# Delta-rule layer in a Trainium2 decoder: chunk solves in four quadrants of the matmul array, with half of the key copies moved by DMA

## The chip, the cores and the metric

One Trainium2 chip, one of its cores. The metric is the device time of one execution of the whole program, in microseconds (us), shown as the median of 3 runs.

## What is computed

The reference is a two-layer decoder on x of 4 sequences x 512 tokens x 128. Each of its six blocks adds its output to x and normalises. The change touches the fourth block only, the delta rule (a linear attention with 16 heads of width 64 and a state matrix W per head):

```python
Q = (x @ Wq).reshape(B, T, H, D)
K = (x @ Wk).reshape(B, T, H, D)
V = (x @ Wv).reshape(B, T, H, D)
beta = jax.nn.sigmoid(x @ Wbeta + b_beta)
K = K / jnp.maximum(jnp.linalg.norm(K, axis=-1, keepdims=True), EPS)
def step(W, inp):
    q_t, k_t, v_t, b_t = inp
    pred = jnp.einsum('bhij,bhj->bhi', W, k_t)
    err = v_t - pred
    W_new = W + b_t[..., None, None] * jnp.einsum('bhi,bhj->bhij', err, k_t)
    o_t = jnp.einsum('bhij,bhj->bhi', W_new, q_t)
    return (W_new, o_t)
```

After it come a cross attention (stage E in the kernel) and a mixture of experts (stage F).

## The kernel before

The kernel runs six stages, A to F. In stage D (the delta rule, from about 1085 us to 1590 us of the span) the 512 tokens of a sequence are cut into 8 chunks of 64, and the recurrence is solved chunk by chunk with matmuls. The work comes in 16 **units** u = 0 to 15; a unit is four heads (two pairs of heads) of one sequence with all 8 chunks. Two units share one **key set** m = u // 2 (eight heads).

For a unit, `d_prep_tensor` (L1747) issues on TensorE, in steps that end in `yield`: values and queries, the `corner` and `fold` products that finish the inverse of each 64x64 chunk matrix, `products` (L1765), four `solve` steps (L1795), then four `update` steps (L1807): transitions "da", steps "db", reads "dr", outputs "do". A solve multiplies the inverse of one chunk (tile d_XE) with the 128 columns of that chunk's values and keys (tile d_KV): 8 chunks x 4 heads = 32 matmuls of 64x64 by 128 columns a unit, in fp32; the trace records each fp32 matmul twice, so it shows 64. Even chunks (`half` 0) lie on partitions 0 to 63, odd ones on 64 to 127. In `solve(k)` a matmul reads the partitions of its half and writes PSUM partitions of the same half, so that two 64x64 quadrants of the array, those on its diagonal, can be at work; `k` runs over two pairs p and two heads `par` of a pair, and each k fills one PSUM bank. ScalarE copies each bank to d_UW (`d_prep_scalar`, L1863, wait at L1893). The updates and `products` take their matmuls in the order of TILES (L1461), in which four successive matmuls use four different quadrants; in the updates a PSUM bank takes the matmuls of one row half.

The banks of this stage come from a ring of five (`ringD`, L1458; class Ring, L91): a step that takes a bank waits until the copy out of its last use is done. `d_chain_tensor` (L1971) carries the state d_S from chunk to chunk: a matmul pair per chunk, an addition on VectorE, the next matmul pair.

The order on each engine is set by `weave` (L35), which merges streams of steps in proportion to their lengths, and by `d_order` (L2051), which says which streams run in an **iteration** u: the chain of unit u, the preparation of unit u+1, and others. Odd iterations (1, 3, 5, 7, 9) also hold the key rows of a later key set, with a Newton square root in small operations on VectorE (`d_rows_vector`, L1596); they prepare units 2, 4, 6, 8, 10. Even iterations 2 to 10 hold key transposes (ident x d_KV into d_KT) and Gram products (d_KT x d_KT) of `d_turn_tensor` (L1543); they prepare units 3, 5, 7, 9, 11. Iterations 11 and 12 hold neither; 13 to 15 hold the start of stages E and F. GpSimd inverts 32x32 blocks (`d_inverse_gpsimd`, L1727), one key set in two iterations.

SyncE issues every DMA, in program order. In stage D it issues, per key set, one reset of d_XI with the unit matrix (`d_inverse_sync`, L1684, loop at L2620); after all eight of them `e_load_sync` (L2138: 7 loads of stage E, once unit 11's outputs are used, semaphore d_out) and `f_load_sync` (L2144). TensorE's first use of the stage E loads is in `e_first_tensor` (L2152), the first step of iteration 13.

## Time and profile before

| | |
|---|---|
| median of 3 runs | 1722.1 us (1721.47 to 1723.83) |
| the profiled execution's own time | 1721.14 us |
| its span | 1719.4 us |
| TensorE busy (matmuls) | 1501.6 us, 87% of the span |
| VectorE busy | 1212.3 us, 71% |
| ScalarE busy | 910.1 us, 53% |
| GpSimd busy | 694.4 us, 40% |
| DMA, mean over the span | 41 GB/s |
| mean granted TensorE clock | 0.946 of full speed |

The profiled execution is 1.0 us under the median. Busy shares are averages over stages with different limits; what a change to stage D is worth has to be read from the stretches in which it runs. In the views below, PE is TensorE, DVE is VectorE, ACT is ScalarE, POOL is GpSimd and SP is SyncE; "ps" is PSUM; an arrow points from the inputs to the output.

### The profile page before, as it was taken

How to read it: one execution, taken by the hardware profiler on the slowest of the kernel's cores; microseconds unless marked ns; L12 is line 12 of the kernel's file. 1: busy time of each engine (PE TensorE's matmuls, PEld its weight loads, DVE VectorE, ACT ScalarE, POOL GpSimd, SP SyncE). 2: the span in 40 equal slices, each digit the busy share in tenths (PEclk: the TensorE clock that was granted, in tenths of full speed). 3: DMA queues.
4: the chain of work that ended last, by engine and by line, in shares of the span. 5: the costliest groups of instructions: out<-in, count | busy, mean ns of one | idle time of the engine just before them, and what ended most of it. 6: DMA issues, size and time to landing. Idle time of an engine off the chain costs nothing.

```text
span 1719.4 us, 41752 instructions
## 1 busy us (share of the span) xinstructions
PE 1501.6 (87%) x18044; PEld 808.2 (47%) x18044; DVE 1212.3 (71%) x2245; ACT 910.1 (53%) x1269; POOL 694.4 (40%) x732
## 2 busy tenths in 40 slices
PE   8887888999999999999978877888889899898985
PEld 4222223333334334333424544777777687664442
DVE  7889877988757774767617668575776666474766
ACT  1676675777757675876671433554445544342220
POOL 1111031566555554665570107447675556000000
PEclk8899999999999999999998989999999999879998
DMA  4000003332222331422301000000000001000000
GB/s 154 1 1 1 1 1 111 100 86 80 80 72 71 84 102 38 106 84 72 88 15 64 1 1 13 15 16 16 3 15 16 15 4 51 37 2 1 7 7 13
DMA packets 32408, 70.65 MB, mean 41 GB/s; under 512 B 5328, under 2 KB 7056, under 8 KB 31968
## 3 DMA queue, kind: packets, MB, share of 16 engines
q1 hardware_dynamic: 32224, 67.98, 13.7%
q8 instruction: 142, 2.33, 0.6%
q14 instruction: 42, 0.34, 0.1%
HBM read 47.45 MB, written 20.51 MB: 40 GB/s over the span
## 4 chain that ended last, share of the span: by engine, by line
PE 57%; DVE 28%; ACT 8%; issue 6%; POOL 1%; DMA 0%; SPq 0%; ACTq 0%; DVEq 0%; POOLq 0%
PE ps L159 55%; DVE a_MX L407 5%; DVE b_mx L863 2%; ACT b_X L923 1%; PE ps L227 1%; PE ps L1551 1%; DVE st L171 1%; DVE sq L206 1%; ACT d_L L168 1%; DVE b_rd L1033 1%; DVE b_VL L798 1%; DVE d_XE L1674 1%; DVE d_KV L1628 1%; POOL b_EL L941 1%; DVE st L197 1%
## 5 line engine op out<-in xcount | busy, mean ns | idle before, releaser
L941 POOL TENSOR_TENSOR b_EL<-b_X,b_EH 128x1024 f16<-128x1024 f32 x160 | 341.2, 2133 | 235.5 <-ACT b_EH L168 235.5
L923 ACT ACTIVATE b_X<-ps 128x1024 f32<-128x1024 f32 x160 | 163.6, 1022 | 118.6 <-PE ps L159 117.2
L1737 POOL TENSOR_TENSOR d_tmp<-d_G,d_XI 128x31 f32<-128x31 f32 (+15 forms) x248 | 128.5, 518 | 194.4 <-DVE d_G L1666 175.6
L863 DVE TENSOR_REDUCE b_mx<-ps 128x2 f32<-128x1024 f32 x128 | 156.0, 1219 | 52.4 <-PE ps L159 50.7
L168 ACT ACTIVATE b_EH<-b_X 128x1024 f16<-128x1024 f32 x160 | 169.1, 1057 | 34.4 <-PE ps L159 23.2
L159 PE MATMUL ps<-b_M,b_S 128*128 128x512 f16 (+1 forms) x768 | 178.4, 386 | 2.4 <-ACT b_X L923 2.4
L407 DVE TENSOR_REDUCE a_MX<-ps 128x2 f16<-128x1024 f32 x128 | 155.3, 1226 | 28.8 <-PE ps L159 27.5
L444 ACT ACTIVATE a_E<-ps 128x1024 f32<-128x1024 f32 x128 | 131.1, 1024 | 77.1 <-PE ps L159 76.4
L1740 POOL TENSOR_TENSOR d_XI<-d_XI,d_tmp 128x31 f32<-128x31 f32 (+15 forms) x248 | 140.8, 568 | 19.4
L426 POOL TENSOR_TENSOR a_QS<-a_QS,a_MR 128x512 f16<-128x512 f16 x16 | 18.5, 1154 | 217.2 <-ACT a_MR L168 213.2
L159 PEld LDWEIGHTS ps<-b_M,b_S 128*128 128x128 f16 (+1 forms) x768 | 55.3, 98 | 101.2 <-issue 40.4
L2474 POOL TENSOR_TENSOR f_Y<-X,f_bo 128x512 f32<-128x512 f32 x4 | 6.1, 1534 | 210.2 <-DVE X L219 112.7
L159 PE MATMUL ps<-b_Hk,b_Hq 64*128 64x154 f16 (+1 forms) x512 | 67.7, 312 | 16.0 <-DVE b_mx L863 15.0
L159 PE MATMUL ps<-f_XM,f_Wh 128*128 128x512 f16 x256 | 78.0, 387 | 0.0
L159 PE MATMUL ps<-a_QS,a_KS 32*128 32x512 f16 x256 | 51.9, 402 | 29.4 <-DVE a_MX L407 29.1
L159 PE MATMUL ps<-d_KV,d_XE 64*64 64x128 f32 x1024 | 72.9, 290 | 1.5 <-issue 1.4
L168 ACT ACTIVATE d_UW<-ps 128x512 f32<-128x512 f32 x64 | 38.2, 597 | 67.3 <-PE ps L159 67.3
L159 PE MATMUL ps<-a_E,a_VA 128*32 128x512 f32 x512 | 73.2, 645 | 0.3
L1346 ACT ACTIVATE c_SG<-ps 128x512 f32<-128x512 f32 x36 | 21.5, 597 | 92.0 <-PE ps L159 88.4
L159 PE MATMUL ps<-b_EH,b_VH 128*64 128x512 f16 x320 | 65.6, 406 | 5.0 <-ACT b_OT L168 2.5
L1002 DVE TENSOR_TENSOR b_den<-b_den,ps 128x512 f32<-128x512 f32 x44 | 30.1, 684 | 51.6 <-PE ps L159 51.3
L159 PEld LDWEIGHTS ps<-b_Hk,b_Hq 64*128 64x128 f16 x512 | 19.9, 94 | 98.3 <-issue 46.7
(324 smaller groups left out, 3435.0 us busy)
## 6 DMA issues: line engine op xcount, KB each, us to landing
b_S<-s_xk SPq DMA_DIRECT2D x48, 336.0 KB, 6.5
b_M<-s_xq SPq DMA_DIRECT2D x48, 256.0 KB, 5.1
s_xk<-b_Hk SPq DMA_DIRECT2D x16, 336.0 KB, 2.2
s_xk<-b_Lk SPq DMA_DIRECT2D x16, 336.0 KB, 2.4
s_xq<-b_Hq SPq DMA_DIRECT2D x16, 256.0 KB, 2.0
s_xq<-b_Lq SPq DMA_DIRECT2D x16, 256.0 KB, 2.0
d_XI<-eye SPq DMA_DIRECT2D x8, 512.0 KB, 3.6
f_w<-f_w SPq DMA_DIRECT2D x1, 2048.0 KB, 7.9
```

Source lines behind the costliest of these rows:

```text
L159: return e.matmul(out, lhsT, rhs, start=start, stop=stop, skip_group_check=True)
L168: return e.activation(out, a, ACT.Copy)
L407: v.e.tensor_reduce(out, PS[:, bk:bk + 2, :], AX, ALU.max).then_inc(sem("a_mx"), 1)
L426: p.e.tensor_tensor(a_QS[G % 4], a_QS[G % 4], a_MR[G % 2], ALU.add).then_inc(sem("a_q2"), 1)
L444: a.e.activation(a_E[c][:, 2 * hp:2 * hp + 2, :], PS[:, bk:bk + 2, :], ACT.Exp, scale=float(D) ** -0.5).then_inc(sem("a_ex"), 1)
L863: last = v.e.tensor_reduce(b_mx[:, 0, :, n], PS[:, bk:bk + 2, :], AX, ALU.max)
L923: a.e.activation(b_X[k % 2], PS[:, bk:bk + 2, :], ACT.Exp, scale=0.125).then_inc(sem("b_ex"), 1)
L941: last = p.e.tensor_tensor(b_EL[k % 6], b_X[k % 2], b_EH[k % 6], ALU.subtract)
L1002: last = v.e.tensor_tensor(b_den[b % 2], b_den[b % 2], PS[:, bk, :], ALU.add)
L1346: a.e.activation(c_SG[n % 3], PS[:, bank["cgu", b, p], :], ACT.Silu).then_inc(sem("c_sl"), 1)
L1737: e.tensor_tensor(tm, a, x, ALU.mult).then_inc(*p.step())
L1740: last = e.tensor_tensor(z, z, tm, ALU.subtract)
```

## The change

- `solve` takes a pair of heads at once: two banks, one per head, and per chunk pair four matmuls in the four quadrants. The first head's results lie as before; the second head's (`par` 1) lie with their halves swapped: even chunks on partitions 64 to 127, odd ones on 0 to 63. There are two solves a unit in place of four, each of 32 / 2 = 16 matmuls with a `yield` in its middle.
- The semaphore d_um rises by 2 a unit and not by 4. ScalarE waits for a whole pair and then makes its two copies.
- `products` writes the second head's results with swapped halves too, and the updates read swapped halves. The four quadrants of an update stay four different ones; their order changes, and a bank now takes matmuls of both row halves.
- The updates' keys of the second heads must lie swapped as well: a new tile d_KW (4 KB on each partition, one buffer) is filled once per key set by `d_swap_sync`: 8 DMAs from SBUF to SBUF, each 64 partitions x 4 heads x 64 words, 64 in all. SyncE waits before them for the keys (d_kn), for the previous key set's last use in "db" (d_bm) and for c_dm.
- TensorE waits for d_kw ahead of the transitions of each key set.
- On SyncE the swap of key set m stands behind the reset of d_XI of key set m + 2, and the last two swaps stand ahead of the loads of stages E and F.
- d_KW takes the place of two buffers of f_XM of stage F; those move to words 5124 on, where the query weights were, with a wait for all queries (d_qm).

```diff
+        d_KW = Room(nc, 34468).take("d_KW", 1024).rearrange("p (c a n) -> p c a n", c=4, a=4)
...
-            v.wait_ge("d_um", 8 * m)
+            v.wait_ge("d_um", 4 * m)
...
+        def d_swap_sync(s, m):
+
+            s.wait_ge("d_kn", 4 * m + 4)
+            s.wait_ge("d_bm", 2 * m)
+            s.wait_ge("c_dm", 16)
+            for c in range(4):
+                for half in range(2):
+                    dma(s.e, "d_kw", d_KW[HALF[1 - half], c], d_KV[m % 3][HALF[half], c, 1, 1:8:2, :])
...
-                    last = mm(e, PS[HALF[half], bk[par], o:o + 64], KT[HALF[par], 2 * j + p, tok(c, half)],
+                    last = mm(e, PS[HALF[half ^ par], bk[par], o:o + 64], KT[HALF[par], 2 * j + p, tok(c, half)],
...
-            def solve(k):
-                par, p = k // 2, k % 2
-                bk = ringD.take(t, ("du", u, k), 1, "d_u", 4 * u + k + 1)
+            def solve(p):
+                bk = [ringD.take(t, ("du", u, p, par), 1, "d_u", 4 * u + 2 * p + par + 1) for par in range(2)]
...
                 for c in range(4):
-                    for half in range(2):
-                        last = mm(e, PS[HALF[half], bk, 128 * c:128 * c + 128], X[HALF[half], at_chunk(p, c, par), :],
+                    for half, par in ((0, 0), (1, 0), (0, 1), (1, 1)):
+                        last = mm(e, PS[HALF[half ^ par], bk[par], 128 * c:128 * c + 128], X[HALF[half], at_chunk(p, c, par), :],
                                   KV[HALF[half], c, :, 4 * j + head(p, par), :])
+                    if c == 1:
+                        yield
                 last.then_inc(sem("d_um"), 1)
+                yield
...
-                        last = mm(e, PS[HALF[par], bk[half], o:o + 64], *operands(HALF[half], p, c, par))
+                        last = mm(e, PS[HALF[par], bk[half], o:o + 64], *operands(HALF[half ^ par], p, c, par))
...
             def keys_of(r, p, c, par):
-                return KV[r, c, 1, 4 * j + head(p, par), :]
+                return d_KW[r, c, 2 * j + p, :] if par else KV[r, c, 1, 4 * j + head(p, par), :]
...
-            for k in range(4):
-                solve(k)
-                yield
-            yield
+            for p in range(2):
+                yield from solve(p)
+            yield
+            t.wait_ge("d_kw", 128 * (m + 1))
             update("da", "d_a", "d_am", 64, 128, 1, 6, transitions)
...
-            for k in range(4):
-                a.wait_ge("d_um", 4 * u + k + 1)
-                copy(e, d_UW[:, 4 * k:4 * k + 4, :],
-                     PS[:, bank["du", u, k], :].rearrange("p (i n) -> p i n", i=4)).then_inc(sem("d_u"), 1)
-                yield
+            for p in range(2):
+                a.wait_ge("d_um", 2 * u + p + 1)
+                for par in range(2):
+                    i = at_chunk(p, 0, par)
+                    copy(e, d_UW[:, i:i + 4, :],
+                         PS[:, bank["du", u, p, par], :].rearrange("p (i n) -> p i n", i=4)).then_inc(sem("d_u"), 1)
+                    yield
...
-        for k, word, n in ((0, 36516, 4), (0, 34468, 2), (0, 6148, 2), (1, 13604, 8)):
+        for k, word, n in ((0, 36516, 4), (0, 6148, 2), (0, 5124, 2), (1, 13604, 8)):
...
+                if k == 6:
+                    v.wait_ge("d_qm", 2 * NU)
...
-            for m in range(NH):
-                d_inverse_sync(s, m)
+            for m in range(NH + 2):
+                if m < NH:
+                    d_inverse_sync(s, m)
+                if m > 1:
+                    d_swap_sync(s, m - 2)
```

Three places of the instruction order, before and with the change.

TensorE in iteration 2, where unit 3's solves (d_KV, d_XE) stand among key transposes (ident, d_KV) and Gram products (d_KT). Before:

```order
L1551 MATMUL ps<-ident,d_KV_189 128x128 x4
L159 MATMUL ps<-d_KV_188,d_XE 64x128 [waits d_pt]
L159 MATMUL ps<-d_KV_188,d_XE 64x128 x7
L1551 MATMUL ps<-ident,d_KV_189 128x128 [waits d_pt]
L1551 MATMUL ps<-ident,d_KV_189 128x128 x3
L159 MATMUL ps<-d_KT_191 64x64 [waits d_kt,d_u]
L159 MATMUL ps<-d_KT_191 64x64 x31
...
L159 MATMUL ps<-d_KT_191 64x64 [waits d_kt,d_g]
L159 MATMUL ps<-d_KT_191 64x64 x31
L159 MATMUL ps<-d_KV_188,d_XE 64x128 [waits d_g]
L159 MATMUL ps<-d_KV_188,d_XE 64x128 x7
```

With the change:

```order
L1552 MATMUL ps<-ident,d_KV_189 128x128 [waits d_pt]
L1552 MATMUL ps<-ident,d_KV_189 128x128 x3
L159 MATMUL ps<-d_KV_188,d_XE 64x128 x8
L1552 MATMUL ps<-ident,d_KV_189 128x128 [waits d_pt]
L1552 MATMUL ps<-ident,d_KV_189 128x128 x3
L159 MATMUL ps<-d_KT_191 64x64 [waits d_kt,d_u]
L159 MATMUL ps<-d_KT_191 64x64 x31
...
L159 MATMUL ps<-d_KT_191 64x64 [waits d_kt,d_g]
L159 MATMUL ps<-d_KT_191 64x64 x31
L159 MATMUL ps<-d_KV_188,d_XE 64x128 x8
```

Each group of 8 solve matmuls stays where it was; eight of them are now two fours of quadrants, and the Gram products still wait for a copy d_u and the copies d_kt.

ScalarE at the same place: copies of transposed keys (d_KT) and of solved chunks (d_UW), then the block copies of d_L. Before:

```order
L168 ACTIVATE d_KT_191<-ps 128x512 [waits d_ptm,d_gm,d_ktp]
L168 ACTIVATE d_UW<-ps 128x512 [waits d_um]
L168 ACTIVATE d_KT_191<-ps 128x512 [waits d_ktp]
L168 ACTIVATE d_UW<-ps 128x512 [waits d_um]
L168 ACTIVATE d_KT_191<-ps 128x512 [waits d_ktp] x2
L168 ACTIVATE d_UW<-ps 128x512 [waits d_um] x2
L168 ACTIVATE d_L_193<-d_L_193 32x32x32 [waits d_g]
```

With the change:

```order
L168 ACTIVATE d_KT_191<-ps 128x512 [waits d_ptm,d_gm,d_ktp]
L168 ACTIVATE d_UW<-ps 128x512 [waits d_um]
L168 ACTIVATE d_KT_191<-ps 128x512 [waits d_ktp]
L168 ACTIVATE d_UW<-ps 128x512
L168 ACTIVATE d_KT_191<-ps 128x512 [waits d_ktp] x2
L168 ACTIVATE d_UW<-ps 128x512 [waits d_um]
L168 ACTIVATE d_UW<-ps 128x512
L168 ACTIVATE d_L_193<-d_L_193 32x32x32 [waits d_g]
```

The order is the same; the first and the third copy of d_UW now wait for a whole pair, so the second d_KT copy stands behind a wait for 16 matmuls and not for 8.

SyncE's queue ahead of the loads of stage E, as a piece of the difference:

```order
+L174 DMA d_KW<-d_KV_187 64x4x64 [waits d_bm,d_kn]
+L174 DMA d_KW<-d_KV_187 64x4x64 x7
+L174 DMA d_KW<-d_KV_189 64x4x64 [waits d_bm,d_kn]
+L174 DMA d_KW<-d_KV_189 64x4x64 x7
+L174 DMA d_KW<-d_KV_188 64x4x64 [waits d_bm,d_kn]
+L174 DMA d_KW<-d_KV_188 64x4x64 x7
 L174 DMA e_wy<-y_wy 128x128 [waits d_out]
 L174 DMA e_cT<-ctx_T 128x616
```

The load of e_wy stood behind the last reset of d_XI; it now stands behind the swap of key set 7, whose wait d_bm is for unit 13.

## Rows read from the trace of the kernel before

**Rows 1.** The page: busy time of the engines, and the chain that ended last.

```profile
PE 1501.6 (87%) x18044; PEld 808.2 (47%) x18044; DVE 1212.3 (71%) x2245; ACT 910.1 (53%) x1269; POOL 694.4 (40%) x732
...
PE 57%; DVE 28%; ACT 8%; issue 6%; POOL 1%; DMA 0%; SPq 0%; ACTq 0%; DVEq 0%; POOLq 0%
```

**Rows 2.** Stretches: length, busy PE, PEld, DVE, ACT, POOL, then PEclk, DMA share, GB/s.

```profile
1200.00:1300.00 100.00, 89.12 (x2624) 73.70 (x2622) 68.85 (x151) 49.06 (x85) 62.61 (x112) 0.98 0.03 9
1524.40:1537.60 13.20, 13.09 (x109) 8.36 (x107) 10.98 (x29) 7.47 (x15) 0.00 (x0) 0.50 0.00 1
```

**Rows 3.** Tile d_KV: all solve matmuls, duration min/median/max in ns.

```profile
L159 PE MATMUL ps<-d_KV,d_XE x1024: 267/269/473, 1095.0 to 1535.5; 64*64 64x128 f32 x171
```

**Rows 4.** Timeline of TensorE in iteration 4 (unit 5): start, length in us, operation.

```profile
1233.02 1.09 PE L159 MATMUL ps<-d_KV,d_XE 64*64 64x128 f32 x16
...
1236.23 1.16 PE L159 MATMUL ps<-d_KT 64*64 64x64 f32 x64
...
1242.05 0.94 PE L159 MATMUL ps<-d_KV,d_UW 64*64 64x64 f32 x48 [0.32 <-ACT d_UW L168]
...
1246.75 2.05 PE L159 MATMUL ps<-d_wo,d_OT 128*128 128x128 f32 x16
```

**Rows 5.** Timeline of ScalarE in the same iteration.

```profile
1234.16 0.60 ACT L168 ACTIVATE d_UW<-ps 128x512 f32<-128x512 f32 x1 [0.43 <-PE ps L159]
...
1235.77 0.60 ACT L168 ACTIVATE d_UW<-ps 128x512 f32<-128x512 f32 x1 [0.43 <-PE ps L159]
...
1241.31 0.60 ACT L168 ACTIVATE d_UW<-ps 128x512 f32<-128x512 f32 x1 [1.21 <-PE ps L159]
1241.80 2.11 ACT L168 ACTIVATE d_L<-d_L 32x1024 f32<-32x1024 f32 x2
```

**Rows 6.** Timeline of TensorE in iteration 5 (unit 6).

```profile
1268.26 1.92 PE L159 MATMUL ps<-d_KV,d_XE 64*64 64x128 f32 x32
1270.71 0.45 PE L159 MATMUL ps<-d_S,d_AT 64*64 64x64 f32 x8 [0.54 <-DVE d_S L2017]
```

**Rows 7.** Timeline of VectorE in iteration 5: the two idle times around the solves.

```profile
1263.18 0.69 DVE L1610 TENSOR_REDUCE d_z<-d_sqk 128x8 f32<-128x512 f32 x1 [1.46 <-ACT d_sqk L1575]
...
1281.59 0.76 DVE L171 SCALAR_TENSOR_TENSOR d_KV<-ps,d_sb 128x256 f32<-128x256 f32 x2 [0.91 <-PE ps L159]
```

**Rows 8.** Timeline of TensorE in iteration 11 (unit 12).

```profile
1428.44 1.85 PE L159 MATMUL ps<-d_KV,d_XE 64*64 64x128 f32 x30
...
1431.17 0.93 PE L159 MATMUL ps<-d_KV,d_UW 64*64 64x64 f32 x48 [0.31 <-ACT d_UW L168]
```

**Rows 9.** Units 0 and 1: TensorE's solves of unit 0, VectorE ahead of unit 1's transitions.

```profile
1095.03 4.95 PE L159 MATMUL ps<-d_KV,d_XE 64*64 64x128 f32 x64
...
1129.38 1.15 DVE L1953 TENSOR_TENSOR d_AT<-d_id,ps 128x192 f32<-128x192 f32 x4 [0.83 <-PE ps L159]
```

**Rows 10.** TensorE from unit 13's steps to the first use of stage E's loads.

```profile
1454.15 0.22 PE L159 MATMUL ps<-d_UW,d_KV 64*64 64x64 f32 x1
...
1459.29 0.68 PE L159 MATMUL ps<-e_cT,e_wy 128*128 128x308 f32 x2
...
1461.90 0.79 PE L159 MATMUL ps<-e_cT,e_wy 128*128 128x308 f32 x2 [1.92 <-ACT d_OT L168]
```

**Rows 11.** SyncE's issues: start and length on the queue, or ns min/median/max.

```profile
1436.92 0.33 SPq L174 DMA_DIRECT2D e_wy<-y_wy  x1
...
1439.90 0.43 SPq L174 DMA_DIRECT2D e_mr<-mask_r  x1
...
L174 SPq DMA_DIRECT2D b_S<-s_xk x48: 574/607/1446, 271.2 to 843.6; - x48
```

**Rows 12.** DMA view of 1436 to 1443 us: packets, MB, share of 16 engines; a load's landing.

```profile
q1 hardware_dynamic: 1008, 0.89, 46.9%
...
e_mr<-mask_r SPq DMA_DIRECT2D x1, 308.0 KB, 3.0
```

**Rows 13.** VectorE in iteration 4: the second transpose that frees a reset of d_XI.

```profile
1250.60 1.22 DVE L1674 STREAM_TRANSPOSE d_XE<-d_XI 128x512 f32<-128x512 f32 x1
```

More of the change, by code:

```diff
@@ L30 @@
     "f_bm": ("a_oc", 16), "f_xm": ("a_pv", 64),
-    "d_inv": ("a_ws", 4), "d_x1": ("b_kv", 6), "d_btm": ("b_kt", 6), "xr_E": ("xr_A", 4), "xr_F": ("xr_B", 4), "f_wh": ("d_wh", 3),
+    "d_inv": ("a_ws", 4), "d_x1": ("b_kv", 6), "d_btm": ("b_kt", 6), "xr_E": ("xr_A", 4), "xr_F": ("xr_B", 4), "f_wh": ("d_wh", 3), "d_kw": ("b_pm", 144),
 }
```

## The prediction

> **What bounds the kernel now.** I read the page first: TensorE is busy 87% of the span and carries 57% of the chain that ended last, VectorE 28% [rows 1]. That is an average. In a stretch of stage D alone TensorE is busy 89 of 100 us, VectorE 69, ScalarE 49, GpSimd 63 [rows 2], so TensorE time looks worth saving; but every engine waits in turn for another there, because the order is fixed and a chunk's results pass from TensorE over ScalarE or VectorE back to TensorE. What a shorter solve is worth must therefore be read unit by unit: which wait ends last behind the solves. For that I went through the timelines of TensorE, ScalarE and VectorE around the solves of all 16 units.
>
> **The solves themselves.** Sixteen records, which are 8 matmuls or 4 diagonal pairs, take 1.09 us, the last of them a duration of 0.27 [rows 3, 4]: (1.09 - 0.27) / 4 = 0.205 us a pair. Thirty-two records give the same, (1.92 - 0.27) / 8 = 0.206 [rows 6]. That two do run side by side is seen beside full-array fp32 matmuls of the same 128 columns, 8 in 2.05 us, 0.22 to 0.25 each [rows 4]. Four quadrants at once are shown by the Gram products: 32 matmuls of 64 columns in 1.16 us, eight fours of about 0.12 [rows 4]. A four of 128 columns thus costs between 0.205 (the pair's rate) and 2 x 0.12 = 0.24; I take 0.21, since the pair has the same columns. A unit goes from 16 x 0.205 = 3.3 us to 8 x 0.21 = 1.7 us (at the other end 1.9): 1.6 us less, 26 us over 16 units. The rest of the working is what of this reaches the end.
>
> **What gives it back: the last copy.** The transitions wait for all four d_UW copies. Before, one copy was left when the last solve ended; now two are, and the second starts some 0.57 us later (copies of 0.60 us, one behind the other [rows 5]). So a unit in which nothing else binds gains 1.6 - 0.6 = 1.0 us.
>
> **Unit by unit.**
> - Units 12 and 13: no key rows, no transposes; TensorE waits 0.31 us for d_UW ahead of the transitions and for nothing else [rows 8]. 1.0 us each: 2.0 (ends 1.6 and 3.0).
> - Units 3, 5, 7, 9, 11, among the transposes. First solve piece at 1233.02, Gram product at 1236.23 [rows 4]. The second piece was done when the second d_UW copy began, at 1235.77 [rows 5]; both pieces shrink by 0.41 us, so it is now done at about 1234.9. ScalarE's first d_UW copy, at 1234.16 before [rows 5], waits for that and stands ahead of the second d_KT copy, which follows 0.57 us later and ends at 1236.05; the Gram product waits for it: about 0.2 us earlier than before, not 1. The same happens in the second half; d_L's copies, which VectorE and the reads wait for, start behind the last d_UW copy (1241.31 before) [rows 5]. I get 0.3 us a unit, 1.5 in all (ends 0 and 5).
> - Units 2, 4, 6, 8, 10, beside the key rows. VectorE has no idle time listed from 1263.18 to 1281.59, a stretch that encloses unit 6's solves; TensorE even waits 0.54 us for an addition that is queued behind VectorE's Newton steps [rows 6, 7]. A faster solve there makes that wait longer. 0.2 a unit, 1.0 in all (ends 0 and 5).
> - Unit 0: 64 records take 4.95 us, as its first part ran at the lower clock [rows 3, 9]; half of that less 0.6 is 1.8 (ends 1.0 and 2.0). Unit 1: VectorE idles only 0.83 us ahead of the transitions [rows 9], so 0.8 at most; I take it (other end 0.4).
> - Unit 14: two normalisation and softmax chains of stage E lie around it; 0 (other end 0.8).
> - Unit 15: TensorE is busy 13.09 of 13.20 us at a granted clock of 0.50, the lower of the two levels, 1.2 GHz; VectorE is busy 10.98 [rows 2]. Its solves cost twice as much and halve to about 3.6 us less, but VectorE has just 2.2 us to give, and ScalarE's mask copies now queue between the two last d_UW copies. 1.5 (ends 0 and 3).
>
> Sum of the gains: 2.0 + 1.5 + 1.0 + 1.8 + 0.8 + 0 + 1.5 = 8.6 us.
>
> **The DMAs.** The swap of a key set is 8 issues on SyncE. No row shows an issue of 64 x 4 pieces; a plain load's takes 0.33 to 0.43 us, and the nearest, a 64 x 2 x 1344 one, has a median of 0.607 and a maximum of 1.446 [rows 11]. I take 0.6, the row nearest in shape. The data are 2048 packets of 256 bytes, 128 on each of 16 engines. Loads of mixed sizes took 0.469 x 7 x 16 / 1008 = 0.052 us a packet [rows 12], so at most some 6.7 us, overlapped with the issues. A swap can start when VectorE's second transpose has freed d_XI, at about 1251.8 [rows 13], and unit 6's transitions come near 1271: 19 us of cover against 0.33 + 8 x 0.6 + 3 = 8 us, and 15 us at the dearest issue. Cost nothing. If that cover were gone, TensorE would stand at d_kw with everything behind it.
>
> **Where a queue does cost: the loads of stage E.** Before, they were issued from 1436.92 to 1440.3, the last landing 3.0 us later [rows 11, 12], far ahead of their first use at 1459.29 [rows 10]. Now the swap of key set 7 stands ahead of them, and it waits for unit 13's steps, which end at 1454.4 [rows 10]. With an issue cost x the loads land at 1454.4 + 8x + 3.4 (their own seven issues) + 3.0. TensorE and VectorE both stand there; nothing between the steps and that use gets shorter. The second of these matmuls before had to wait until 1461.90 anyway, for a bank [rows 10]; that part of the stall was already paid. The net loss is (1454.4 + 8x + 6.4 + 0.65) - 1461.9 = 8x - 0.45: at x = 0.6 4.4 us, at 0.33 2.2, at 1.446 11.1. The loads of stage F follow a few us later and are used 50 us on: nothing. The two moved f_XM buffers wait for queries that are issued before: nothing.
>
> **The sum.** 8.6 - 4.4 = 4.2 us less than the profiled execution's 1721.1, 1716.9. The median of the runs is 1.0 us above that execution; on its scale I predict **1718 us**.
>
> **Rivals.**
> 1. *The load queue eats the gain* (the slower side). One mechanism: SyncE's eight issues ahead of the stage E loads. From x = (8.6 + 0.45) / 8 = 1.1 us an issue the change is no gain; at 1.446 and gains of 3 to 8 us it ends at 1724 to 1730. For it: the four 256-byte pieces per partition; the maximum of the nearest row. Against: its median. 0.25.
> 2. *The units beside key rows and transposes gain more*, because VectorE's and ScalarE's work moves up with TensorE's. At 0.8 a unit in place of 0.2 and 0.3, 5 to 6 us more: 1712. For it: those engines are idle at many other places. Against: the waits of [rows 5 to 7]. 0.20.
> 3. *The four quadrants don't run four wide.* A bank now takes both row halves at once, in the solves and the updates. If they then ran in pairs, solves would stay as they are, and an update of 24 matmuls, 0.94 us now [rows 4], would double: about 3 us a unit, 1722 + 16 x 3 = 1770. Against: the solves of before put both halves into one bank, and paired [rows 3, 4]. This is a rule of the Trainium skill, TensorEngine Tiling (Array Packing), section Restrictions and Gotchas: "Different row tiles cannot access same PSUM bank simultaneously", with the synchronisation left to software. The trace of before disagrees as far as timing goes, for two quadrants; no row shows four with two banks. 0.05.
> 4. *The swaps land late* for the transitions. It takes 2 us or more an issue; every further us is paid seven times. 1730 and up. 0.04.
>
> **How the numbers follow.** The forecast, some 3 to 8 us faster or near it, has 0.46; its own range is 1713 to 1721. The measurement tells 0.2% (3.4 us) from no change, so faster is below 1718.7 and slower above 1725.5. Of the forecast's 0.46 I put 0.28 below 1718.7, with rival 2 that makes 0.48; slower has 0.05 + 0.04 and 0.13 of rival 1, 0.22; the rest, 0.30, is the same. The bounds would reach from 1722.1 - 20 + 2.2 = 1704 to 1722.1 - 3 + 11.1 = 1730; leaving out the outermost parts and rivals 3 and 4, the range is 1709 to 1728.
>
> **What the profile after would show.** Solve records: 64 in about 2 us of TensorE time a unit in place of 3.5, and the updates' 24 matmuls still 0.94 us (if 1.8, rival 3). Behind the solves of units 12 and 13 the wait for d_UW should be 0.7 to 0.9 us and not 0.31. In iteration 4 TensorE should wait ahead of the Gram product for d_KT, and in iteration 5 for d_S. SyncE's rows give x directly, and the wait for the loads of stage E should be 5 to 7 us once; none for d_kw. The prediction is wrong if x is far from 0.6, if units beside key rows gain more than 0.5 us each, or if a new wait shows at each key set.

## The result and the profile after

| | before | after |
|---|---|---|
| median of the runs | 1722.1 us (5 runs, 1720.32 to 1724.11) | 1731.2 us (5 runs, 1729.90 to 1732.03) |
| profiled execution, span | 1719.4 us | 1728.1 us |
| mean granted TensorE clock | 0.946 | 0.942 |

The ratio is 1.0057, with a 95% interval of 1.0045 to 1.0070: slower by some 9 us, where I had forecast 4 faster. A second measurement, with 12 runs (below), gave 1.0039 (1.0021 to 1.0056).

The page of after, busy times and chain, against [rows 1]:

```profile
PE 1482.0 (86%) x18044; PEld 785.3 (45%) x18044; DVE 1212.5 (70%) x2245; ACT 905.9 (52%) x1269; POOL 695.7 (40%) x732
...
PE 53%; DVE 28%; ACT 8%; issue 7%; POOL 3%; DMA 1%; SPq 1%; ACTq 0%; DVEq 0%; POOLq 0%
```

TensorE is busy 19.6 us less, from 1501.6, and its share of the chain falls from 57% to 53%. The work did get shorter; the span did not. So waits grew by more than the work shrank, and GpSimd, a DMA and SyncE's queue stand in the chain with 3, 1 and 1%.

**Where it went.** The most useful yardstick was the start of each unit's `d_AT` subtraction on VectorE, which is one event per unit. The differences between such starts, from the profiles of before and after:

| stretch | before | after | after less before | forecast |
|---|---|---|---|---|
| start to unit 0 | 1101.74 | 1099.98 | -1.8 | -1.8 |
| unit 0 to 2 | 58.69 | 59.60 | +0.9 | -1.0 |
| unit 2 to 11 | 249.36 | 249.76 | +0.4 | -2.3 |
| unit 11 to 13 | 43.48 | 42.20 | -1.3 | -2.0 |
| unit 13 to 14 | 40.71 | 48.87 | +8.2 | +4.4 |
| unit 14 to 15 | 45.80 | 46.77 | +1.0 | -1.5 |
| unit 15 to the end | 179.6 | 180.9 | +1.3 | 0 |

A stretch between two such starts holds the work of the later unit. The last two columns add up to +8.7 and -4.2 us.

How far can one profile be trusted? Five kernels (some of them described below) have the same TensorE work up to unit 13 (after and runs 1, 3, 9 and 10). Their profiles give 248.9 to 250.1 us for units 2 to 11, but 41.5 to 44.7 us for units 11 to 13. The latter goes with the clock: from unit 11 to 12 they took 21.1 to 21.4 us where the granted clock was 1.00, 23.0 us at 0.85 and 24.4 us at 0.79. Before took 22.4 us there at 0.92, after 21.1 at 1.00, so part of the -1.3 us is the clock. The start of unit 0 lies between 1096.0 and 1100.2 us in these five, so the -1.8 us in the first line is no measurement of unit 0.

Two things are to be explained: nine units with 1.6 us less TensorE work each that gain nothing, and 8 us lost at one place.

**Nine units that gain nothing.** Groups of TensorE's instructions between the subtractions of units 2 and 11 (busy, mean ns, idle time before them and its releaser). Before:

```profile
L159 PE MATMUL ps<-d_KV,d_XE 64*64 64x128 f32 x576 | 37.2, 272 | 0.7 <-issue 0.7
...
L159 PE MATMUL ps<-d_S,d_AT 64*64 64x64 f32 x432 | 23.7, 226 | 5.1 <-DVE d_S L2017 2.9 <-issue 1.8
...
L159 PE MATMUL ps<-d_KT 64*64 64x64 f32 x640 | 11.6, 221 | 0.0
...
L159 PE MATMUL ps<-d_KV,d_UW 64*64 64x64 f32 x432 | 8.7, 222 | 1.8 <-ACT d_UW L168 1.6
```

After:

```profile
L159 PE MATMUL ps<-d_S,d_AT 64*64 64x64 f32 x432 | 24.1, 227 | 11.0 <-DVE d_S L2031 9.5 <-issue 1.0
L159 PE MATMUL ps<-d_KV,d_XE 64*64 64x128 f32 x576 | 22.7, 276 | 0.4 <-issue 0.4
...
L159 PE MATMUL ps<-d_KT 64*64 64x64 f32 x640 | 11.6, 221 | 4.5 <-ACT d_KT L168 4.5
...
L159 PE MATMUL ps<-d_KW,d_UW 64*64 64x64 f32 x216 | 9.4, 222 | 4.2 <-ACT d_UW L168 4.2
```

The solves fell from 37.2 to 22.7 us, 14.5 / 9 = 1.6 us a unit, as forecast. What came back: the recurrence's waits for `d_S` +6.6, the Gram products' for `d_KT` +4.5 (from none), the updates' for `d_UW` +2.6 (from 1.6). That is 13.7 of the 14.5 us. These are idle times before TensorE's instructions, and not yet causes: the experiments show that the first of the three comes with any shorter solve, and only the other two with the late signal (table behind run 7).

Iteration 4 shows how, on ScalarE of after, against [rows 5]:

```profile
1233.79 0.60 ACT L168 ACTIVATE d_UW<-ps 128x512 f32<-128x512 f32 x1 [1.22 <-PE ps L159]
1234.29 0.59 ACT L168 ACTIVATE d_KT<-ps 128x512 f32<-128x512 f32 x1
1234.76 0.60 ACT L168 ACTIVATE d_UW<-ps 128x512 f32<-128x512 f32 x1
1235.24 0.62 ACT L168 ACTIVATE d_KT<-ps 128x512 f32<-128x512 f32 x1
1237.26 0.60 ACT L168 ACTIVATE d_KT<-ps 128x512 f32<-128x512 f32 x1 [1.40 <-PE ps L1552]
1239.66 1.08 ACT L168 ACTIVATE d_UW<-ps 128x512 f32<-128x512 f32 x2 [1.80 <-PE ps L159]
```

ScalarE idles 1.22 us at the first `d_UW` copy with a `d_KT` copy queued behind it. TensorE, on its side, then stands for that `d_KT` (timeline of the same iteration, against [rows 4]):

```profile
1231.87 0.67 PE L159 MATMUL ps<-d_KV,d_XE 64*64 64x128 f32 x16
...
1233.06 0.67 PE L159 MATMUL ps<-d_KV,d_XE 64*64 64x128 f32 x16
...
1235.02 1.16 PE L159 MATMUL ps<-d_KT 64*64 64x64 f32 x64 [0.71 <-ACT d_KT L168]
```

A piece that TensorE does in 0.67 us is a signal only at the end of the second piece. The copies are not slow (0.60 us as before); they are let go late, and both of a pair at once.

**Eight microseconds at one place.** SyncE's issues and TensorE in after, against [rows 10, 11]:

```profile
1452.73 6.17 SPq L174 DMA_DIRECT2D d_KW<-d_KV  x8
1458.95 0.60 SPq L174 DMA_DIRECT2D e_wy<-y_wy  x1
...
1461.97 0.43 SPq L174 DMA_DIRECT2D e_mr<-mask_r  x1
```

```profile
1456.91 0.82 PE L159 MATMUL ps<-d_wv,d_XS 128*128 128x256 f16 x6
1465.04 2.42 PE L159 MATMUL ps<-e_cT,e_wy 128*128 128x308 f32 x4 [7.31 <-DMA e_mr<-mask_r]
```

The eight swap issues take (1458.95 - 1452.73) / 8 = 0.78 us each on average, the loads of stage E are issued 22 us later than before, and TensorE stands 7.31 us, VectorE 6.40. The average hides two kinds of issue. Three of the eight, from the chain that ended last, and all 64 by tile (duration in ns, min/median/max):

```profile
1456.08 0.62 SPq L174
...
1456.74 1.50 SPq L174
...
1458.29 0.62 SPq L174
...
L174 SPq DMA_DIRECT2D d_KW<-d_KV x64: 590/617/1914, 1084.8 to 1458.3; - x64
```

The usual issue takes 0.62 us, with 0.04 us to the next; one of the eight took 1.50.

The matmuls behind the stall take 2.42 us for four records where they took 0.68 and 0.79 for two each. The stretch between units 13 and 14 falls into three parts: up to the first matmul on the loads, that group of matmuls, and the rest. The last two, before and then after (length, busy PE, PEld, DVE, ACT, POOL, then PEclk, DMA share, GB/s):

```profile
1459.29:1462.69 3.40, 1.48 (x8) 0.57 (x8) 1.60 (x5) 3.36 (x5) 0.00 (x0) 1.00 1.00 328
1462.69:1493.98 31.29, 27.03 (x526) 21.14 (x526) 15.42 (x49) 10.60 (x20) 0.00 (x0) 0.89 0.08 32
```

```profile
1465.04:1467.46 2.42, 2.42 (x6) 1.24 (x8) 1.02 (x3) 0.00 (x0) 0.00 (x0) 0.50 0.94 215
1467.46:1500.41 32.95, 28.80 (x527) 22.08 (x526) 15.42 (x48) 10.16 (x19) 0.00 (x0) 0.77 0.14 58
```

The first part grew from 6.02 to 13.50 us, by 7.5. The second shrank by 1.0: its wait for a bank is gone, but right after the standstill the granted clock is 0.50, the lower level of 1.2 GHz, and the matmuls take 0.9 us more. The third grew by 1.7 us, with as many matmul records (527 and 526) and 1.8 us more TensorE time for them, at a granted clock of 0.77 in place of 0.89.

### The profile page after: what moved, and what is told of

It reads as the page before. It is cut to its first block, busy times and chain, and to the rows that moved or that the text cites. A ratio compares the mean times of both kernels' runs of the same rounds, so it can differ in the third digit from the quotient of the medians.

```text
span 1728.1 us, 41836 instructions
## 1 busy us (share of the span) xinstructions
PE 1482.0 (86%) x18044; PEld 785.3 (45%) x18044; DVE 1212.5 (70%) x2245; ACT 905.9 (52%) x1269; POOL 695.7 (40%) x732
## 4 chain that ended last, share of the span: by engine, by line
PE 53%; DVE 28%; ACT 8%; issue 7%; POOL 3%; DMA 1%; SPq 1%; ACTq 0%; DVEq 0%; POOLq 0%
PE ps L159 51%; DVE a_MX L407 5%; DVE b_mx L863 2%; ACT b_X L923 1%; POOL d_XI L1750 1%; POOL d_tmp L1747 1%; DVE st L171 1%; PE ps L227 1%; DVE sq L206 1%; ACT d_L L168 1%; DVE b_rd L1033 1%; DVE d_zb L171 1%; POOL b_EL L941 1%; DVE st L197 1%; DVE st L186 1%
## 5 line engine op out<-in xcount | busy, mean ns | idle before, releaser
L159 PEld LDWEIGHTS ps<-b_M,b_S 128*128 128x128 f16 (+1 forms) x768 | 55.6, 98 | 102.3 <-issue 41.5
L159 PE MATMUL ps<-d_S,d_AT 64*64 64x64 f32 x768 | 45.5, 235 | 19.7 <-DVE d_S L2031 16.9
```

The costliest lines, as they stand in the source:

```text
L159: return e.matmul(out, lhsT, rhs, start=start, stop=stop, skip_group_check=True)
```

## The experiments

Twelve kernels ran, in four groups, each group beside runs of the kernel before on its own chip; the medians of before were 1719.8, 1721.8, 1722.9 and 1723.0 us. So ratios are compared, not medians, and a time that an expectation names has to be read as a distance from before's. Where a stretch between units is given, it is from the one profiled execution.

**1. The loads of stage E ahead of the last swap.**

```diff
+                if m == NH + 1:
+                    e_load_sync(s)
                 if m > 1:
                     d_swap_sync(s, m - 2)
-            e_load_sync(s)
```

> The changed kernel, with the seven loads of stage E issued on SyncE ahead of the swap of key set 7 instead of behind it; nothing else moves. In the changed kernel they are issued from 1458.95 us and the last lands at about 1465.0, and between the start of unit 13's transitions' subtraction (1451.54) and that of unit 14 (1500.41) lie 48.9 us, 8.2 more than before. Theory Q (queue): the loss is that queue; with the loads early the interval goes back to 40.5 to 42 us, and the time from 1731.2 to 1722 to 1724. Rival S (swap traffic or the split copies slow stages D and E wherever they stand): the interval stays at 45 us or more, the time at 1728 or more. Rival C (the low clock after the stall is a matter of its own): part comes back only, 1725 to 1728, with a granted clock under 0.8 still seen between 1475 and 1500.

Measured: 1723.6 us, ratio 1.0027 (1.0012 to 1.0042). Units 13 to 14 took 41.55 us, as theory Q said, and no engine waited for a load. But on the ratio some 5 us above before are left, more than theory Q's 0 to 2: the queue is one cause, not the only one. Rival C's sign, a granted clock under 0.8 between 1475 and 1500 us, is not clearly there (0.80), and the stretch is within 0.9 us of before's, so what is left lies elsewhere. A part of it shows in unit 15, which took 46.74 us as in after. ScalarE and VectorE there (clock 0.50):

```profile
1528.98 0.60 ACT L168 ACTIVATE d_UW<-ps 128x512 f32<-128x512 f32 x1 [10.42 <-PE ps L159]
1529.48 1.08 ACT L168 ACTIVATE f_mk<-ps 128x512 f16<-128x512 f32 x2
```

```profile
1530.10 1.30 DVE L2433 TENSOR_TENSOR f_XM<-f_XHL,f_mk 128x1024 f16<-128x1024 f16 x2 [2.91 <-ACT f_mk L168]
```

Before, the same first copy started at 1526.38, and VectorE waited 0.19 us for the masks:

```profile
1527.54 1.29 DVE L2417 TENSOR_TENSOR f_XM<-f_XHL,f_mk 128x1024 f16<-128x1024 f16 x2 [0.19 <-ACT f_mk L168]
```

Mask copies that have nothing to do with the solves stand behind the `d_UW` copy on ScalarE, and VectorE, with 11 us of work to do in 13 [rows 2], stands 2.9 us for them.

**2. The swaps alone.** The kernel before with `d_swap_sync`, its wait on TensorE, the moved `f_XM` buffers and the loads of stage E behind the last swap; nobody reads `d_KW`.

```diff
+                if m > 1:
+                    d_swap_sync(s, m - 2)
             e_load_sync(s)
...
+            t.wait_ge("d_kw", 128 * (m + 1))
             update("da", "d_a", "d_am", 64, 128, 1, 6, transitions)
```

> The kernel before with the swap DMAs alone: eight issues a key set on SyncE as in the changed kernel, TensorE's wait for them ahead of the transitions, the moved mask buffers; the solves, products and updates stay in their old two-quadrant order and nobody reads the swapped keys. Theory Q: stage D runs as before up to unit 13 (starts of the subtractions within 0.5 us of before, 1453.3 for unit 13); then the loads land at 1454.4 + 6.2 + 3.4 + 3.0 = 1467.0, 5 to 6 us late, and what follows the stall adds some 2 to 3: 1729 to 1732. Rival S: units 2 to 11 already lag, by 1 us or more a key set, and the whole is 1735 or more. Rival (the four quadrants themselves cost the time): within 3 us of before, 1722 to 1725.

Measured: ratio 1.0049 (1.0032 to 1.0066), 8.4 us slower. Units 2 to 11 took 249.43 us (before 249.36), units 13 to 14 49.01 us. The 8.3 us of that stretch are as much as the whole difference by the ratio. In the profile units 0 to 2 took 1.4 us less than before and units 11 to 13 2.7 more, with a granted clock of 0.80 from unit 11 to 12; unit 13 began at 1455.2 and not at 1453.3. With no four-quadrant matmul in the kernel, the stall costs what it costs in after.

**3. The changed kernel with one swap.** Swaps of key sets 1 to 7 left out, and TensorE's wait for them.

```diff
-                if m > 1:
-                    d_swap_sync(s, m - 2)
+                if m == 2:
+                    d_swap_sync(s, 0)
```

> The changed kernel with the swap of key set 0 alone; the swaps of key sets 1 to 7 are left out, so that from unit 2 on the odd heads' transitions and steps are computed with key set 0's swapped keys. It prices the swaps as DMAs. Theory Q: the loads of stage E are early again and nothing else changes, so the time is that of the run with early loads within 1 us, 1722 to 1724, and unit starts up to unit 13 are within 0.5 us of the changed kernel's. Rival S: it is faster than the run with early loads by 2 us or more, and the gain shows from unit 2 on.

Measured: ratio 1.0025 (1.0010 to 1.0039), the same as run 1; units 2 to 11 249.19 us. The transfers themselves cost nothing that these runs can tell, which is some 4 us; their place in front of other loads does.

**4. Half the solves**, in the kernel before.

```diff
-                for c in range(4):
+                for c in range(0, 4, 2):
```

> The kernel before with half of the solves' matmuls left out (chunks 2, 3, 6 and 7 of every head are not solved, so what follows uses stale numbers); semaphores, copies and order are those of before. TensorE's solve goes from 3.3 to about 1.7 us a unit, as with four quadrants, but with one copy left behind the last solve, not two, and with no DMAs. It asks what a shorter solve is worth. Theory W (in units 2 to 11 other waits end last: VectorE's queue, the copies of the turned keys, GpSimd's inverse): 0.0 to 0.4 us a unit there, 1.2 to 1.6 in units 0, 12, 13 and 15: 1714 to 1719. Rival L (the copies that were pushed back are what ate it): 1.2 to 1.6 us in nearly every unit: 1698 to 1705.

Measured: ratio 0.9945 (0.9926 to 0.9963), 9.5 us faster, and units 2 to 11 took 240.71 us, 8.7 us less. In just those units in which I saw other waits end last, a shorter solve is worth nearly 1.0 us a unit, if the copies stay where they were. That is over twice the 0.4 us that theory W, which was mine, gives at most, and less than rival L's 1.2; the median, too, lies between the two. Other waits do take part of the gain: the solves of these nine units fell by 15.8 us, from 37.2 to 21.4.

**5. Finer pieces**, on top of run 1.

```diff
-            def solve(p):
-                bk = [ringD.take(t, ("du", u, p, par), 1, "d_u", 4 * u + 2 * p + par + 1) for par in range(2)]
+            def solve(k):
+                p, q = k // 2, k % 2
+                bk = [ringD.take(t, ("du", u, k, par), 1, "d_u", 8 * u + 2 * k + par + 1) for par in range(2)]
...
-                for c in range(4):
+                for c in (2 * q, 2 * q + 1):
...
-                    if c == 1:
-                        yield
                 last.then_inc(sem("d_um"), 1)
...
-            for p in range(2):
-                a.wait_ge("d_um", 2 * u + p + 1)
+            for k in range(4):
+                a.wait_ge("d_um", 4 * u + k + 1)
                 for par in range(2):
```

Each of the two copies is then of 128 x 256, and the updates wait for eight of them (edits of offsets and wait values left out here).

> The run with early loads, and the solves signalled in four pieces a unit again: a piece is two chunks of both heads of a pair, 16 matmuls in four quadrants, written to half of two banks, and ScalarE copies each piece with two copies of 128 x 256 as soon as it is done; the updates still wait for all. Theory P (pair waits: the changed kernel signals once a pair, so ScalarE's first copy, and whatever stands behind it on ScalarE, starts a piece late, and two copies of 0.6 us are left behind the last solve): most of what the half solves gained comes back, 0.5 to 0.9 us a unit, and 1 us more in unit 15, where VectorE waited 2.9 us for a mask copy: 1712 to 1718 on the scale where the run with early loads has 1723.6 and the kernel before 1719.8. Theory W (other waits end last, whatever the copies do): 1722 to 1725. Rival B (twice as many bank takes from a ring of five, and 0.15 us more of copies a piece): slower than the run with early loads.

Measured: ratio 0.9957 (0.9939 to 0.9975), 1713.1 us where before had 1721.8. It beats both kernels. TensorE's wait for `d_KT` between units 2 and 11 is 0.9 us (4.5 in after), and iteration 4 on ScalarE reads

```profile
1233.31 0.60 ACT L168 ACTIVATE d_KT<-ps 128x512 f32<-128x512 f32 x1 [2.53 <-PE ps L1552]
1233.94 0.66 ACT L168 ACTIVATE d_UW<-ps 128x256 f32<-128x256 f32 x2
1234.49 0.60 ACT L168 ACTIVATE d_KT<-ps 128x512 f32<-128x512 f32 x1
```

with no idle time ahead of the first `d_UW` copy. The time is in theory P's range, but not by its sum: units 2 to 11 took 247.70 us, 1.7 less than in run 1 or 0.2 us a unit, where P said 0.5 to 0.9. Between the starts of units 0 and 15 the profile is 9.3 us shorter than that of run 1; 1.5 of that is unit 15, where P said 1, and 6.0 are in units 1, 2 and 12 to 14, in part by a higher granted clock (0.92 against 0.85 from unit 11 to 12).

**6. The pair waits alone**, in the kernel before.

```diff
-                a.wait_ge("d_um", 4 * u + k + 1)
+                a.wait_ge("d_um", 4 * u + 2 * (k // 2) + 2)
```

> The kernel before, with one edit: ScalarE's copies of the first and second solve of a head pair wait for the second, those of the third and fourth for the fourth. No DMAs, no four quadrants, solves as long as before. It prices the pair waits alone. Theory P: the last two copies stand behind the last solve, 0.6 us later a unit, and the first a solve of 0.8 us later: 0.4 to 0.8 us a unit, 6 to 12 us in all, 1726 to 1732 where the kernel before has 1719.8. Theory W: nothing, 1718 to 1722.

Measured: ratio 1.0104 (1.0080 to 1.0127), 18 us slower, over 1 us a unit and more than the theory that came nearest. Units 2 to 11 took 257.12 us, 7.8 more.

**7. Half solves and pair waits together.** The edits of runs 4 and 6.

> The half solves (13.6 us less between the first and the last unit in the profile, 11 us less in the times) with the pair waits of the run before this one: solves as short as with four quadrants and copies as late as in the changed kernel, but without its DMAs, key swap and quadrant order. Theory P: the pair waits swallow most of that gain; 1717 to 1722, that is 8 or more above the half solves alone. Theory Q2 (four quadrants or the swapped keys cost something of their own, and the waits do not): it stays at 1708 to 1712.

Measured: ratio 0.9978 (0.9959 to 0.9997). The pair waits take back 0.0033, that is 5.7 us, of the 9.5, under the 8 that theory P said. In the profiles units 2 to 11 took 244.27 us, 3.6 more than in run 4, unit 15 46.62 us, 2.6 more, and all from unit 0 to 15 8.6 more. Theory P in direction; the two measures leave the size open.

TensorE's idle time between units 2 and 11 in us, by what ended it ("issue" is idle time for which the profile shows no wait):

| kernel | units 2 to 11 | d_S | d_KT | d_UW | issue |
|---|---|---|---|---|---|
| before | 249.36 | 5.3 | 0.0 | 1.6 | 7.2 |
| run 6, pair waits | 257.12 | 2.7 | 3.4 | 5.4 | 9.5 |
| run 4, half solves | 240.71 | 12.3 | 1.0 | 1.6 | 1.7 |
| run 7, both | 244.27 | 11.6 | 4.4 | 4.0 | 2.5 |
| after | 249.76 | 12.5 | 4.5 | 4.2 | 7.3 |
| run 5, finer pieces | 247.70 | 11.1 | 0.9 | 2.0 | 9.4 |

The pair waits bring the waits for `d_KT` and `d_UW`, with long solves as with short ones, and the finer pieces take them away again. The wait for `d_S`, VectorE's addition in the recurrence, rises by some 5 to 7 us in every kernel with short solves, whatever the copies do: so much of a shorter solve is lost to it, and that is what was right in theory W.

**8. Finer pieces, loads late.** Run 5 without the edit of run 1.

> The changed kernel with the finer pieces alone; the loads of stage E stand behind the swap of key set 7 again. With the changed kernel, the early loads and both together it makes a square. If the two causes are separate: the early loads were worth 5 to 8 us without the finer pieces and should be worth the same with them, so this one is 5 to 8 us above the run with both (ratio to before 0.9957), that is 0.3% faster to 0.1% slower than before. If the stall hides what the pieces gain (TensorE waits for the same landing however early it comes there): the units before the stall give nothing, and the ratio is 1.002 or more.

Measured: ratio 1.0000 (0.9986 to 1.0014), in the range of separate causes. Units 13 to 14 took 46.77 us where run 5 had 38.73.

**9. The last swap in sixteen issues**, in the changed kernel; TensorE's wait for it is set to match.

```diff
...
+                        for j in range(2):
+                            dma(s.e, "d_kw", d_KW[HALF[1 - half], c, 2 * j:2 * j + 2], d_KV[m % 3][HALF[half], c, 1, 4 * j + 1:4 * j + 4:2, :])
```

> The changed kernel with the last swap, of key set 7, in sixteen issues of two heads each in place of eight of four; all else as in the changed kernel. Theory Q: SyncE's queue sets when the loads of stage E land, so eight more issues of 0.6 to 0.8 us come on top: 5 to 6 us on the wait of 7.3 us for the last load, and 5 to 6 us on the time. If an issue's time goes by its packets and not by the issue (half the pieces, half the time), nothing changes: within 1 us of the changed kernel. If the stall were the clock or VectorE's queue rather than the landing: under 3 us.

Measured: ratio 1.0076 (1.0056 to 1.0097), 6.1 us above the changed kernel of the same group. SyncE's queue and TensorE:

```profile
1451.63 11.18 SPq L174 DMA_DIRECT2D d_KW<-d_KV  x16
```

```profile
1469.10 2.42 PE L159 MATMUL ps<-e_cT,e_wy 128*128 128x308 f32 x4 [12.47 <-DMA e_mr<-mask_r]
```

11.18 / 16 = 0.70 us an issue with half the packets in each. Again one was long. Three of them, from the chain:

```profile
1454.87 0.61 SPq L174
...
1455.53 1.43 SPq L174
...
1457.00 0.61 SPq L174
```

In the chain 15 of the 16 take 0.59 to 0.62 us and one 1.43, as in after seven take 0.59 to 0.70 and one 1.50. So the usual issue costs the same 0.61 us with half the packets: the price is the issue's. Five microseconds more of queue are five more of stall (7.31 to 12.47) and five more between units 13 and 14 (54.05).

**10. The changed kernel again.** No edit.

> The changed kernel itself, beside the others on the same chip, for a comparison with as many runs as theirs: ratio to before 1.0045 to 1.007 as first measured; the interval between the subtractions of units 13 and 14 at 48 to 49.5 us, units 2 to 11 within 0.5 us of before's 249.4 us in all.

Measured: ratio 1.0039 (1.0021 to 1.0056), a little under the first measurement. Units 13 to 14 took 49.42 us, units 2 to 11 250.11, 0.2 us more than expected.

The square, as ratios to before:

| | loads late | loads early |
|---|---|---|
| signal once a pair | 1.0039 (first measured 1.0057) | 1.0027 |
| finer pieces | 1.0000 | 0.9957 (repeated: 0.9931) |

Finer pieces are worth 0.0039 and 0.0070; early loads 0.0012 (or 0.0030) and 0.0043. Each ratio has an interval of 0.0014 to 0.0026 to either side, so that neither the size of one edit to better than some 4 us nor an interplay of the two is settled, and the 0.0012 alone is within the noise. The stretch between units 13 and 14 is clearer: early loads shorten it by 7.3 to 7.9 us in the first row (48.87 and 49.42 to 41.55) and by 8.0 in the second.

**11. Half the columns**, in the kernel before: as many solve matmuls as ever, with 64 columns each.

```diff
-                        last = mm(e, PS[HALF[half], bk, 128 * c:128 * c + 128], X[HALF[half], at_chunk(p, c, par), :],
-                                  KV[HALF[half], c, :, 4 * j + head(p, par), :])
+                        last = mm(e, PS[HALF[half], bk, 128 * c:128 * c + 64], X[HALF[half], at_chunk(p, c, par), :],
+                                  KV[HALF[half], c, 0, 4 * j + head(p, par), :])
```

> The kernel before with all of its solve matmuls, but 64 columns each instead of 128 (the keys' halves of the products are left out, so the transitions and steps use stale ones). The half solves had half the matmuls and took 8.7 us off units 2 to 11, where the finer pieces, with as many matmuls as before, took off 1.7 us. This one tells the two apart: TensorE's time for the solves is about halved while the number of its instructions stays. Theory N (what the units gain hangs on how many instructions TensorE has to take in, whose idle time put down to issue was 1.7 us with half solves and 9.4 with finer pieces): units 2 to 11 gain 0 to 3 us, and the time is 1714 to 1719. Theory K (the columns count, and what the finer pieces lose again is in their eight copies, their bank takes or the swap): 6 to 9 us, and 1707 to 1712.

Measured: ratio 0.9938 (0.9917 to 0.9960), units 2 to 11 242.21 us, 7.2 less than before. Theory K: the number of instructions matters little, 1.5 us against run 4. TensorE's idle time put down to issue was 5.9 us between units 2 and 11, against 1.7 with half the matmuls.

**12. Early loads and finer pieces again.**

> The early loads and the finer pieces once more, beside the run above on the same chip: ratio to before 0.994 to 0.9975 as first measured, units 2 to 11 together 247 to 248.5 us, and 38.5 to 40.5 us between the subtractions of units 13 and 14.

Measured: ratio 0.9931 (0.9906 to 0.9957), 1711.3 us, a little better than the range expected; units 2 to 11 247.80 us, units 13 to 14 39.88. The better version stands.

## Why the prediction was wrong

By its own steps:

- **The solves**: 3.3 to 1.7 us a unit. Right in the difference: 1.6 us a unit, from 37.2 to 22.7 us in nine units. Rival 3 is out: a solve piece of 16 records takes 0.67 us where it took 1.09, and an update of 48 records, 0.94 to 1.02 us long before, takes 0.93 to 1.09. Of the rule of the Trainium skill, TensorEngine Tiling (Array Packing), section Restrictions and Gotchas, that different row tiles cannot use one bank at the same time, this kernel shows no cost in the solves' own length: two quadrants of different row halves, written to one bank's two partition halves, ran as fast as computed. Read as a rule for whole banks, it is contradicted as far as time goes; read as one for the same partitions of a bank, no kernel here tries it, since no two matmuls that run together write them.
- **The last copy's 0.6 us a unit**. This is the step that failed, as far as the runs show it. I took it off only where nothing else bound, units 0, 12 and 13, and for the rest went by the waits of before, each with a small gain and an end of the range at 0; my sum had no way to lose anything in a unit. But the same edit also holds back the first copy and whatever is queued behind it on ScalarE, and that has a price in units where the shorter solve gains. Run 6 prices the pair waits alone at 18 us with long solves, run 7 at 5.7 us with short ones (8.6 in the profiles). "Nothing too" was no lower end: a gain of 8.7 us that was there for units 2 to 11 (run 4) ended as -0.4. Of the 9.1 us between the two, 3.6 are the pair waits' (run 7); the other 5.5 came with the four quadrants and stay open, as said below.
- **Units 3 to 11, 0.3 us; 2 to 10, 0.2 us.** I had read the right rows and drawn the wrong sum. The forecast that TensorE would wait for `d_KT` in iteration 4 and for `d_S` in iteration 5 came true (0.71 us; 1.42 and 0.76 us ahead of the recurrence around unit 6's transitions). I had it as the reason why a gain is small, and did not ask whether the wait comes from the solves' length or from the signal's place. It is the length for `d_S` and the place for `d_KT` (table behind run 7).
- **Units 12 and 13, 1.0 us each.** 1.3 us in both together, 1.8 in the repetition, but partly by the clock: before had 0.92 from unit 11 to 12 where these two had 1.00. Where the clocks match, unit 12 took 24.4 us in run 3 against 25.6 in run 2, which has the old solves, and unit 13 20.1 to 21.1 us in the five changed kernels against 20.5 and 21.1. That makes 1.2 us and some 0.4. The wait for `d_UW` was 0.84 us, inside the 0.7 to 0.9 that I gave.
- **Units 0 and 1.** In the profiled execution the lead at the start of unit 1's subtraction was 2.0 us (2.6 forecast) and shrank to 0.85 us at unit 2's, 32.23 us on where it had been 31.05. The chain of after runs through GpSimd there: it finishes the second key set's inverse at 1132.33, 0.57 us before the 1132.90 of before, with a lead of 2 us elsewhere. This is read from the traces and was not tried. That is the 3% of GpSimd in the chain, and in none of my rivals.

```profile
1132.36 1.24 DVE L1675 STREAM_TRANSPOSE d_XE<-d_XI 128x512 f32<-128x512 f32 x1 [3.28 <-POOL d_XI L1750]
```

- **Unit 15, 1.5 us gain.** It lost 1.0, and 0.9 in each of runs 1, 3, 9 and 10. I had named the cause, the mask copies queued with `d_UW` copies on ScalarE, and let it make the gain smaller but not turn it. Runs 4 and 7 differ in the pair waits alone: 44.05 and 46.62 us.
- **Behind unit 15, nothing.** It lost 1.3 us more, 0.9 to 1.2 in runs 1, 3, 9 and 10 and 1.0 in run 7. I had no term for it, and no run looks for its cause.
- **The swaps' 0.** Right: no wait for `d_kw`, and run 3 leaves them out with no gain.
- **The loads of stage E, net 4.4 us.** The mechanism was right, the size was not, though the 8.2 us lie within the ends that I gave, 2.2 and 11.1. The wait came out at 7.3 us against 5 to 7. The usual issue took the 0.6 us that I said; one of 1.50 us and the 0.04 us between issues make the average x 0.78, and by the formula 8 x 0.78 - 0.45 = 5.8 us. The remaining 2.4 stand behind the stall, where I had written that nothing gets shorter and had not asked what gets longer. The two pairs of matmuls right behind the stall took 2.42 us at a granted clock of 0.50 and not 1.48, and the work from there to unit 14 took 1.8 us more TensorE time at 0.77 in place of 0.89. The first belongs to the stall: those matmuls take 2.42 us in all five kernels that stall (after, runs 2, 8, 9 and 10) and 1.5 in runs 1, 3, 5 and 12, which do not. The second is less clear: without any stall that part of the stretch is 32.1 us in run 1 and 31.2 in run 3, where before has 31.3 and after 33.0, and the longer stall of run 9 makes it no longer (33.0). VectorE idles 6.4 us at the same landing:

```profile
1465.02 0.48 DVE L2185 TENSOR_SCALAR e_mk<-e_mr 128x616 f32<-128x616 int32 x1 [6.40 <-DMA e_mr<-mask_r]
```

So the mechanism of rival 1, the load queue, is what made the kernel slower, below the break-even of x = 1.1, because the gains it was set against were not 8.6 us but about 0. In the profile the forecast is off by 12.9 us: 3.8 at the loads and 9.1 in the gains, of which 2.7 in units 2 to 11, 2.5 in unit 15, 1.9 in units 1 and 2, 0.7 in units 12 and 13 and 1.3 behind unit 15.

**What stays open.** With solves of the same length, the four-quadrant kernels need some 5.5 us more between units 2 and 11 than their two-quadrant counterparts: 249.8 against 244.3 us with pair waits (after, run 7), 247.7 against 242.2 with copies by piece (run 5, run 11). The swaps are not it (run 3, 249.2), nor is it the number of instructions alone (run 11). In both pairs the four-quadrant kernel has more TensorE time (206.5 against 203.1 us, 209.9 against 207.3) and more idle time put down to issue (7.3 against 2.5, 9.4 against 5.9), and less of some other waits; before has 7.2 us of the latter too. The two banks that a piece takes at once are a candidate, and so are the swapped order of the updates and, for the pair of run 5 only, its eight shorter copies. None was tried.

## What to carry to other kernels

When work is regrouped so that two results finish together, price the signal as well as the work: the first consumer starts later, the last has two to do, and everything queued behind the first waits too. Test that in isolation, as one changed wait value. And when an in-order DMA queue gets new issues that wait for something late, list what stands behind them: here seven loads had landed some 16 us ahead of their first use, and all of that was gone because of where eight issues, 6.2 us together, were put; that the transfers cost anything no run shows.

## What the runs showed of the hardware

- An issue of 64 rows of 4 pieces of 256 bytes took 0.62 us on SyncE's queue (median of 64), with 2 pieces 0.61 us, and plain loads mostly 0.33 to 0.43 us. Halving the packets did not shorten the issue. Among the eight or sixteen issues of the last swap one took 1.4 to 1.5 us, so that the average was 0.78 and 0.70 us.
- Four quadrants of 64 x 64 with two banks and 128 columns did run side by side: 16 records took 1.09 us in pairs, 0.67 us in fours.
- A stall costs more than its length: 7.3 us of standing made the interval 8.2 us longer, though the wait of 1.9 us for a bank fell away. Right after it the granted clock was 0.50, and four records took 2.42 us that took 1.48 us at 1.00.
